# Where the Q and V projections stand among the attention units of a causal attention block

## The reference

```python
Q, K, V = heads(x @ WQ.T), heads(x @ WK.T), heads(x @ WV.T)
scores  = where(causal, Q @ K^T / sqrt(64), -1e9)
attn    = softmax(scores)
x = layernorm(x + concat(attn @ V) @ WO.T)
x = layernorm(x + ffn(x))   # rms norm, 8-bit quantization per token,
                            # times an int8 weight matrix, plus bias
```

## Time and profile before

| | us |
|---|---|
| median of three runs | 1737.63 |
| the profiled execution, its own time | 1737.58 |
| its span, slowest core (core 3) | 1735.8 |
| spans of the eight cores | 1731.3 to 1735.8 |
| attention of sequence 0, chunk 0 (with the projections) | 120.3 to 265.5 |
| chunk 1 | 265.5 to 350.7 |
| chunk 2 | 350.7 to 471.7 |
| chunk 3 | 471.7 to 626.7 |
| TensorE busy, share of the span | 72% |
| ScalarE busy | 47% |

### The profile page before, as it was taken

The page is one execution under the profiler, slowest core; times in us unless marked ns, Lnnn a source line. Parts: engine busy times, 40 slices in busy tenths (PEclk is TensorE's granted clock), DMA queues, the critical chain, the costliest instruction groups (busy, mean ns, idle before and its releaser), DMA issues.

```text
span 1735.8 us, 27201 instructions; the slowest of 8 cores (1731.3 to 1735.8 us)
## 1 busy us (share of the span) xinstructions
PE 1251.3 (72%) x8710; PEld 598.7 (34%) x8710; DVE 663.5 (38%) x1775; ACT 807.7 (47%) x1060; POOL 304.7 (18%) x599
## 2 busy tenths in 40 slices
PE   1988987777777785667409889777777777766664
PEld 0433433443443442222204334333343343422221
DVE  1333342211111138888703333422111111488886
ACT  0000026777788743444400000376777887434444
POOL 1000033222211201122200000333122111112112
PEclk9999985556678678888759999855656867788887
DMA  9330033000000001222192300220000000012211
GB/s 165 53 49 0 1 50 49 2 2 1 1 2 2 1 13 61 73 81 85 66 163 42 49 0 1 49 50 1 2 1 1 1 2 1 15 60 89 81 61 61
DMA packets 21924, 64.65 MB, mean 37 GB/s; under 512 B 1315, under 2 KB 1315, under 8 KB 21796
## 3 DMA queue, kind: packets, MB, share of 16 engines
q0 software_dynamic: 17184, 46.14, 13.3%
q1 hardware_dynamic: 4612, 16.78, 3.2%
HBM read 75.50 MB, written 16.78 MB: 53 GB/s over the span
## 4 chain that ended last, share of the span: by engine, by line
PE 38%; DVE 19%; ACT 19%; POOL 9%; issue 7%; DMA 5%; DVEq 1%; ACTq 0%; POOLq 0%
ACT PT L512 17%; PE psall L266 14%; POOL PT L548 9%; PE psall L680 8%; PE psall L336 6%; PE psall L412 5%; DMA wslotB<-wkt 5%; DVE o_ring L600 4%; PE psall L430 4%; DVE dump L718 2%; DVE dumpb L721 2%; DVE OT L467 2%; DVE st L724 1%; DVE st L725 1%; DVE z L881 1%
## 5 line engine op out<-in xcount | busy, mean ns | idle before, releaser
L512 ACT ACTIVATE PT<-psall,ebias 128x1024 bf16<-128x1024 f32 x448 | 484.3, 1112 | 225.4 <-PE psall L412 218.6
L412 PE MATMUL psall<-QT,KT 64*128 64x512 bf16 (+3 forms) x1280 | 302.1, 475 | 139.4 <-DVE OT L467 49.7
L430 PE MATMUL psall<-Vx,PT 128*128 128x65 bf16 x4352 | 311.6, 222 | 58.9 <-POOL PT L548 54.7
L548 POOL TENSOR_TENSOR PT<-PT,mask 128x128 bf16<-128x128 bf16 x512 | 202.6, 425 | 809.9 <-ACT PT L512 665.6
L430 PEld LDWEIGHTS psall<-Vx,PT 128*128 128x128 bf16 x4352 | 220.1, 113 | 229.7 <-issue 215.8
L587 DVE RECIPROCAL rinv<-psall 128x4 f32<-128x4 f32 x64 | 11.6, 182 | 628.6 <-PE psall L430 628.6
L680 PE MATMUL psall<-wslotA,OT 128*128 128x512 bf16 x512 | 158.9, 483 | 79.9 <-DVE z L881 44.6
L523 ACT ACTIVATE PT<-psall,ebias 128x768 bf16<-128x768 f32 (+2 forms) x192 | 131.1, 686 | 169.1 <-PE psall L412 164.5
L266 PE MATMUL psall<-xT,wslotB 128*128 128x512 bf16 x512 | 116.0, 391 | 85.6 <-DMA wslotB<-wkt 85.6
L412 PEld LDWEIGHTS psall<-QT,KT 64*128 64x128 bf16 x1280 | 78.4, 98 | 250.2 <-issue 235.3
L864 PE MATMUL psall<-wslotB,qT 128*128 128x512 bf16 x512 | 123.9, 398 | 42.6 <-ACT qT L848 42.6
(11 more groups left out here) (94 smaller groups left out, 941.7 us busy)
## 6 DMA issues: line engine op xcount, KB each, us to landing
xstg<-x SPq DMA_DIRECT2D x32, 512.0 KB, 3.6
y<-outst POOLq DMA_DIRECT2D x32, 512.0 KB, 3.0
xT<-xt POOLq DMA_DIRECT2D x8, 1024.0 KB, 20.9
wslotB<-wkt POOLq DMA_DIRECT2D x2, 2048.0 KB, 41.1
wslotA<-wqt POOLq DMA_DIRECT2D x2, 2048.0 KB, 52.1
wslotB<-wvt POOLq DMA_DIRECT2D x2, 2048.0 KB, 16.4
wslotA<-wot POOLq DMA_DIRECT2D x2, 2048.0 KB, 16.6
wslotB<-w8t POOLq DMA_DIRECT2D x2, 2048.0 KB, 17.3
```

The lines of the kernel that those rows point to most:

```text
L412: last = eng.matmul(out, lhsT, rhs, start=True, stop=True, skip_group_check=True)
L430: last = eng.matmul(out, lhsT, rhs, start=(i_glob < 2), stop=(i_glob >= n_total - 2), skip_group_check=True)
L512: eng.activation(PT[:, pt * 1024:(pt + 1) * 1024], psall[:, p * 1024:(p + 1) * 1024], AF.Exp, bias=ebias[:, :], scale=0.125).then_inc(sem_ ...
L548: last = eng.tensor_tensor(blk, blk, mask01[:, :], ALU.mult)
```

## The change

The order of the Q and V groups among the units is written anew. The number of groups that must be out after a unit is now a formula for each chunk:

- Chunk 0: two V groups behind each of the first 4 units, 8 in all; then one Q group behind every third unit, 8 in all.
- Before the first unit of chunk 1: 8 V groups in one piece. (The same line stands before chunks 2 and 3 and finds nothing left.)
- Chunk 1: from its 18th unit on, one V group behind every second unit, 16 in all, the last behind unit 48 of 64; one Q group behind every sixth unit, 8 in all.
- Chunk 2: one Q group behind every eighth unit, 8 in all, the last behind unit 64 of 96.

Where both fall on one unit, the Q group comes first. PV now waits in every chunk for the V rows of its key tile, and the last PV of a head, which had no such wait, gets one too. The wait on V at the start of chunks 1 to 3 goes. The load of the int8 weights follows the last V group (the 48th unit of chunk 1), and that of WO the last Q group (the 64th unit of chunk 2).

```diff
             for qc in range(4):
                 for hp in range(8):
-                    if hp == 0 and qc >= 1:
-                        W("t", "v", v_upto[min(4 * qc + 3, 15)])
+                    if qc >= 1 and hp == 0:
+                        while vg_next < min(32, 8 * qc + 8):
+                            emit_vg(vg_next)
+                            vg_next += 1
+                            if vg_next == 32 and w8_done is None:
+                                w8_done = wload2(w8_h, 1, ctr["t"])
...
-                                if qc == 0:
-                                    W("t", "v", v_upto.get(ku))
+                                W("t", "v", v_upto.get(ku))
...
+                        nst = u + 1
                         if qc == 0:
-                            nst = u + 1
-                            while qst["i"] < min(nq, 2 * nst):
-                                emit_qgroup()
-                            if qst["i"] == nq and wo_done is None:
-                                wo_done = wload2(wo_h, 0, P["H"]["q_all"])
-                            while vg_next < min(32, 2 * nst):
-                                emit_vg(vg_next)
-                                vg_next += 1
+                            vtarget = min(8, 2 * nst)
+                            qtarget = min(8, max(0, nst - 4) // 3)
+                        elif qc == 1:
+                            u1 = nst - 32
+                            vtarget = 8 + min(24, u1 // 2)
+                            qtarget = 8 + min(8, u1 // 6)
+                        elif qc == 2:
+                            u2 = nst - 96
+                            vtarget = 32
+                            qtarget = 16 + min(8, u2 // 8)
+                        else:
+                            vtarget = 32
+                            qtarget = 24
+                        while qst["i"] < qtarget:
+                            emit_qgroup()
+                        if qst["i"] == nq and wo_done is None:
+                            wo_done = wload2(wo_h, 0, P["H"]["q_all"])
+                        while vg_next < vtarget:
+                            emit_vg(vg_next)
+                            vg_next += 1
+                            if vg_next == 32 and w8_done is None:
+                                w8_done = wload2(w8_h, 1, ctr["t"])
...
                     if pend:
                         W("t", "g", maskv[u0 + n_kt - 1])
+                        W("t", "v", v_upto.get(n_kt - 1))
                         emit_pv(qc, hp, pend, n_started, n_total)
...
                     if qc >= 1:
-                        while vg_next < 32:
-                            emit_vg(vg_next)
-                            vg_next += 1
-                        if w8_done is None:
-                            w8_done = wload2(w8_h, 1, ctr["t"])
                         emit_trans(qc - 1, hp)
```

## The result

The changed kernel takes 1781.38 us against 1738.81 in the same comparison: a ratio of 1.0245 (95% interval 1.0220 to 1.0271), 42.6 us slower. The forecast was 24.6 us slower. The direction and the main mechanism held; some terms of the sum were too small. Some executions of every kernel run a few per cent longer because part of the cores get a lower clock: ratios leave these out, while the medians given beside them include them (e4's 1705.1 us would be 1703.7 without). The profiled execution is that of the slowest core (core 7), 1779.0 us against a mean of 1768.7 over the cores. Before, all eight lay within 4.5 us; now they lie within 21.

A forecast was written before the change was run, and what follows sets the result against it. No engine fills the span; the limit changes by stage. Fill terms sum to 111.3 us a sequence against 99.0 today, 12.3 more, 24.6 for two: 1737.6 + 24.6 = 1762 us, range 1720 to 1800.

The forecast's parts named there:

- the forecast's own band: Whole kernel: a time of 1745 to 1780 us, chance 0.53.
- rival 2: Chunk 1: V finds no slack and the clock falls between groups, 16 us more a sequence, 1795; above 1780, chance 0.23.
- Lone Q groups: Chunk 0: 8 single Q groups each stop ScalarE and mostly start at a low clock, 24.8 us in all.
- The piece: Before chunk 1: 8 V groups in one piece with nothing covering them, 15.3 us.
- Chunk 1: 2 Q groups before unit 18 cost 7.5 us; 16 V and 6 Q groups in units 18 to 48 cost 27.0.
- Head 0: First head of chunk 0: 8 V groups cost 10.1 us plus 1.4 for start and clock, 11.5.
- Chunk 2: 8 single Q groups cost 16.1 us, plus 8.6 for those that meet the low clock: 24.7.
- The waits: New wait before each head's last PV: 0.14 us each, 4.5 for 32 heads; in mid-head 0.
- The credit of 4.0 for a clock that stays high: After a lone group the clock stays high for a while: 4.0 us taken off in all for a sequence.
- The first rival: Chunks 0 to 2: fill keeps TensorE at 2.4 GHz, 1707 us; in full or in half, chance 0.20.
- The third rival: Groups run under the exps at little cost, Q at 1.3 us too, time about 1690; chance 0.04.

The follow-up runs named there:

- e4: The changed kernel with the 24 remaining Q groups written into V's two PSUM quarters, not the score buffers: 1705.1 us, ratio 0.9740 to the kernel before.
- e2: The changed kernel with V groups back where they were, two behind each of the first 16 units: 1790.1 us, ratio 1.0234 to the kernel before.
- e3: The changed kernel with Q groups back where they were, two behind each of the first 12 units: 1734.8 us, ratio 0.9880 to the kernel before.
- e8: The changed kernel with Q groups in pairs at half as many places: 1732.7 us, ratio 0.9966 to the kernel before.
- e6: Dense schedule in chunks 0 and 1 and few waits, Q groups in the score buffers as in the changed kernel: 1691.0 us, ratio 0.9729 to the kernel before.
- e7: The changed kernel with the 8 V groups before chunk 1 put singly behind every third unit of chunk 0: 1740.7 us, ratio 1.0009 to the kernel before.
- e10: The changed kernel without the new wait before a head's last PV: 1763.7 us, ratio 1.0135 to the kernel before.
- e11: The kernel before with all the new waits on V and nothing else of the change: 1743.1 us, ratio 1.0015 to the kernel before.
- e5: Q groups in V's PSUM quarters, few waits, a dense schedule in chunks 0 and 1: 1613.7 us, ratio 0.9281 to the kernel before.
- e1: The changed kernel with waits on V only in each chunk's first head and none before the last PV: 1768.9 us, ratio 1.0112 to the kernel before.
- e9: The changed kernel again, unaltered, for comparison on the same chip: 1783.7 us, ratio 1.0252 to the kernel before.
- run 192: Not a run label: in e11's profiled execution, cores 4 and 5 run 192 matmuls from 60 to 110 us, granted a clock of 0.81.
- run 227: Not a run label: in e11's profiled execution, the other six cores run 227 to 234 matmuls from 60 to 110 us, at 0.99 to 1.00.

## Why the prediction was right, and where it was too small

The measured 1781 us lies within the range of 1720 to 1800, but 1 us above the forecast's own band, where the chances had put rival 2, whose mechanism didn't come about. The direction and the largest terms held; that chunk 1 came out within 1 us is in part luck, as shown below.

- **Lone Q groups are the loss.** Right, and shown from four sides (e2, e3, e4, e8). In chunk 0 the last seven heads take 67.7 us, less seven bare ones of 5.77 and 1.0 for waits 26.3 for 8 groups, against 24.8. That Q's hold on the score buffer makes the stop was a premise; e4 and e6 show it.
- **The piece.** 15.3 forecast, 15.16 measured. What I didn't see is that the same groups put elsewhere would have been worth more than their length (e7).
- **Chunk 1.** 136.1 forecast, 135.0 measured. The four filled heads take 20.51, 14.28, 14.37 and 20.84 us, 70.0 in all, 27.4 above bare heads where the sum had 27.0. This agreement is partly luck: the sum had 0.9 us for a lone V group, and e3 shows 0.4 in the two middle heads, so other terms there were too low. The two heads with two Q groups cost 20 us above bare ones, the two with one Q group 7. That V groups hold the clock up there was right (0.91), so the second rival falls.
- **Head 0.** 11.5 forecast. The first head ends 20.2 us after its first score matmul, 14.4 above a bare one. TensorE waited 1.63 us for V's weights, and the first pair took 4.96. The old order had covered that load with Q groups, and I counted half of it: 2.9 short. In sequence 1 no such wait shows, the clock is 1.00, and the first head ends 17.29 us after its first score matmul, 11.5 above a bare one, as forecast.
- **Chunk 2.** 25.8 forecast with its waits. Measured 28.4 on the slowest core and 23 to 25 on the others in sequence 0; in sequence 1 28.7 on the slowest and 27 on most others. (The sum's 8.6 for the clock should be 6 x 1.46 = 8.8.)
- **The waits.** 0.14 us was near (0.10), but the product with 64 heads, 9 us, wasn't the price: 20 in this kernel (e10), 3 in the old one (e11). Of the single terms this one is furthest off. A fixed price for each wait was the wrong form for it.
- **The credit of 4.0 for a clock that stays high.** No row of the kernel before gave its size. No chunk shows it either; chunk 3 of sequence 1 is 5.6 us longer (160.15 against 154.54).

By stage, on the slowest cores, the shortfall divides as follows (measured less forecast, each chunk with its 0.14 us a head for the wait):

| us | sequence 0 | sequence 1 |
|---|---|---|
| credit not seen | +4.0 | +4.0 |
| first head | +2.9 | 0.0 |
| other heads of chunk 0 | +1.6 | +1.1 |
| chunk 1 | -1.1 | -0.8 |
| chunk 2 | +2.7 | +2.9 |
| chunk 3 | -1.3 | +4.5 |

The credit is the largest, then chunk 2, chunk 3 and the first head. The rows sum to 20.5 us; outside attention the kernel is 1.0 us shorter, and 18.6 are missing between the spans, the rest being rounding and the spread among heads of the kernel before. The 11 us by which e10 exceeds the priced waits are no further row: they lie within these, on core 0 about half of them in chunk 3.

The first rival (fill lifts the clock and the change gains) is wrong for this schedule and right for a denser one. One group in three units leaves the clock at 0.67; two in three units bring 0.95 (e7), and four in eight, without a break, bring 1.00 (e5). The third rival was right on one point, that Q would be cheap without the buffer conflict, and the change left the conflict in.

The Trainium skill (TensorE: Matmul & The Clock Gate, "HAM oscillation — how this bites in real kernels") advises, for a kernel whose bursts of matmuls are parted by waits for DMA, to restructure the loop so that TensorE stays warm, which means at full clock. The trace agrees where the schedule alone was made dense: e6, with Q in the score buffers as in the changed kernel, has 0.92 over the last seven heads of chunk 0 against 0.67, and is 90 us faster, some 12 of them by its fewer waits (e1).

The Trainium skill (TensorE: Matmul & The Clock Gate, "Seeing it yourself") gives a third clock level of 13/16, 0.81, that a whole die falls to once three or more of its cores run dense matmuls. The runs agree only in part. With all eight cores busy the dense stretches are mostly granted 1.00, in e5 for 88 us in chunk 1. But in the profiled execution of e11 cores 4 and 5 are granted 0.81 from 60 to 110 us, in the projections, and run 192 matmuls there, where the other six cores have 0.99 to 1.00 and run 227 to 234. So the level exists here, on two cores of a die and not on all four; what brought it on isn't shown.

## What to carry to other kernels

Filler for TensorE is cheap only where it takes no buffer that the critical loop turns over; give it its own PSUM before moving it. Spread it evenly and densely enough that the clock stays up and then stop, rather than thinly over everything: a lone group cost 1.2 to 1.5 us even with its own PSUM, against 0.45 to 0.6 in a dense stretch. A wait behind a stall is 0.1 us, but in a loop that swings between two clock levels its effect on the whole was three times its length in one order (e10) and less than half of it in another (e11), so measure it in place.

## What the runs showed that I had not expected

- More work in less time: 8 more V groups in seven heads, 66.9 us down to 62.9, clock 0.67 to 0.95 (e7 against the changed kernel).
- Bare heads with the same work run at different clocks from core to core and kernel to kernel: a head of chunk 3 takes about 19 us where it is granted 0.77 and 20.1 to 20.9 where it is granted 0.50, and the chunk's eight heads together 152.8 to 161.0 us at a mean clock of 0.60 to 0.77. In the changed kernel's order 0.1 us a head moved this mean (e9 against e10).
- A Q group of 1.73 us costs 2.8 to 3.5 us in a score buffer at a low clock, 1.7 there at full clock, 1.2 to 1.5 alone in its own quarters, and 0.45 in a dense stretch.
